# Second attention: weighed sums and the chain behind them moved in a software pipeline on one Trainium2 core

## The reference, cut to what matters

```python
q = query @ q_w + q_b; k = query @ k_w + k_b; v = query @ v_w + v_b
k = concatenate([k, bias_k]); v = concatenate([v, bias_v])        # 129 keys
w = einsum('bth,bsh->bts', q * scaling / 32, k)                   # per head
gate = sigmoid((query_layer @ grep_w + grep_b).sum(-1)) * grep_a
w = w + gate * rel_emb[buckets]
probs = softmax(w); attn = einsum('bts,bsh->bth', probs, v)
x = layernorm(x + attn @ out_w + out_b)
```

## Time and profile before

| what | value |
|---|---|
| median of 3 runs | 5380.33 us (5378.53 to 5382.32) |
| the profiled execution | 5384.48 us, span 5382.7 us |
| PE busy, granted clock over the span | 4154.7 us (77%), 0.77 |
| DVE busy | 3559.9 us (66%) |
| ACT busy | 2231.5 us (41%) |
| POOL busy | 1734.5 us (32%) |
| last `turn_rows` of the block | starts 3321.2 us |

### The profile page before, as it was taken

One profiled execution on the slowest core, in us unless ns is written; L12 is line 12 of the kernel. 1 busy time (PEld: TensorE's weight loads), 2 busy tenths in 40 slices (PEclk: granted clock), 3 DMA queues, 4 the chain that ended last, 5 costly groups with the idle time before them and its releaser, 6 DMA issues. The chain is left out here.

```text
span 5382.7 us, 100296 instructions
## 1 busy us (share of the span) xinstructions
PE 4154.7 (77%) x31987; PEld 2750.2 (51%) x31987; DVE 3559.9 (66%) x9085; ACT 2231.5 (41%) x5050; POOL 1734.5 (32%) x2290
## 2 busy tenths in 40 slices
PE   7878888878885666655989998777773299999998
PEld 3555555555554455443666666666663144444443
DVE  6565655645554555545888887555556688888888
ACT  1444444431111222214777776222221155555555
POOL 1000000015451000004565665000000077777777
PEclk9999999986555555556777776666665599999999
DMA  2000000000000000001000000111111365666664
GB/s 62 9 8 8 8 8 10 8 17 26 27 26 27 23 23 23 23 18 38 15 14 15 15 14 12 29 29 29 30 29 37 92 150 138 137 137 137 137 137 98
DMA packets 261713, 245.06 MB, mean 46 GB/s; under 512 B 28491, under 2 KB 188016, under 8 KB 261490
## 3 DMA queue, kind: packets, MB, share of 16 engines
q1 hardware_dynamic: 252402, 239.73, 18.5%
q10 hardware_dynamic: 9216, 4.20, 0.3%
HBM read 210.27 MB, written 33.55 MB: 45 GB/s over the span
## 5 line engine op out<-in xcount | busy, mean ns | idle before, releaser
L2314 POOL TENSOR_TENSOR d_hidden<-d_gated,d_upper 128x512 f32<-128x512 f32 x528 | 801.8, 1544 | 235.8 <-DVE d_upper L2423 110.5
L2430 DVE TENSOR_TENSOR d_h_low<-d_hidden,d_h_high 128x512 f16<-128x512 f32 x528 | 540.9, 1024 | 118.8 <-ACT d_h_high L2390 117.6
L2384 ACT ACTIVATE d_gated<-d_g 128x512 f32<-128x512 f32 x528 | 315.2, 597 | 468.3 <-PE d_u L2330 468.3
L2423 DVE TENSOR_TENSOR d_upper<-d_u,d_coef 128x512 f32<-128x512 f32 x512 | 349.1, 682 | 35.5 <-DMA d_coef<-coefT 16.3
L2390 ACT ACTIVATE d_h_high<-d_hidden 128x512 f16<-128x512 f32 x528 | 328.4, 622 | 8.2 <-POOL d_hidden L2314 8.2
L1563 ACT ACTIVATE c_sc<-c_sc,c_negmax 128x129 f32<-128x129 f32 x1024 | 326.2, 393 | 12.1 <-issue 9.7
L706 POOL MEMSET f_minus_half<- 128x1 f32 x1 | 0.1, 99 | 1027.4 <-POOLq L37 1027.4
L129 POOL TENSOR_TENSOR b_rstd<-b_var_eps,b_minus_half 128x1 f32<-128x1 f32 x128 | 67.1, 549 | 665.7 <-DVE b_var_eps L119 665.7
L1391 POOL TENSOR_TENSOR c_posg<-w_pos,c_gate 128x512 f32<-128x512 f32 x256 | 265.7, 1039 | 0.0
L2328 PE MATMUL d_g<-d_x_high,w_Wg_high 128*128 128x512 f16 x528 | 200.7, 380 | 79.0 <-DVE d_upper L2423 40.7
L129 POOL TENSOR_TENSOR d_rstd<-d_var_eps,d_minus_half 128x1 f32<-128x1 f32 x64 | 34.0, 547 | 682.0 <-DVE d_var_eps L119 682.0
(11 more groups left out here) (407 smaller groups left out, 11380.3 us busy)
## 6 DMA issues: line engine op xcount, KB each, us to landing
d_coef<-coefT SPq DMA_DIRECT2D x256, 512.0 KB, 7.6
mx_x<-in_xT SPq DMA_DIRECT2D x16, 256.0 KB, 2.8
b_x<-in_x SPq DMA_DIRECT2D x64, 64.0 KB, 1.8
y<-b_y SPq DMA_DIRECT2D x64, 64.0 KB, 1.6
f_y<-y SPq DMA_DIRECT2D x64, 64.0 KB, 1.9
f_x<-in_x SPq DMA_DIRECT2D x64, 64.0 KB, 1.9
x<-f_res SPq DMA_DIRECT2D x64, 64.0 KB, 1.5
b_x<-x SPq DMA_DIRECT2D x64, 64.0 KB, 1.8
```

The costliest lines, as they stand in the source:

```text
L2314: nc.gpsimd.tensor_tensor(hidden[b][:], gated[b][:], upper[b][:], ALU.mult).then_inc(h_ready, 1)
L2384: nc.scalar.activation(gated[b][:], ps_g[i][:], ACT.Silu, scale=1.0 / W_SCALE).then_inc(silu_ready, 1)
L2423: nc.vector.tensor_tensor(upper[b][:], ps_u[i][:], coef[c % CBUFS][:, u % CU, :], ALU.mult).then_inc(upper_ready, 1)
L2430: nc.vector.tensor_tensor(h_low[b][:], hidden[b][:], h_high[b][:], ALU.subtract).then_inc(h_low_ready, 1)
```

## The change: what it does

On PE, `weigh` goes from quarter 3 of the next column (`behind1`) to quarter 1 of the one after (`behind2`), between the turn of quarter 3 and `project`, which so comes behind `scores` and `turn`. `combine` goes to quarter 2, `turn_attn` to quarter 3 and `output` to quarter 0 of `behind3`. On ACT and DVE the parts that belong to them move along. On POOL `power` moves to quarter 1 of `behind3`, and the second product of `choose` becomes `last_values`, behind `low_parts`, with a wait for `pv_ready` of the item 4 places earlier, whose tile it writes over. `bn_stats` counts on a semaphore of its own, `bn_ready`, instead of the shared one.

```diff
@@ POOL @@
                     nc.gpsimd.tensor_tensor(chosen[s][:], following_kv[s][:, 1], own_next, ALU.mult).then_inc(chosen_ready, 1)
-                    nc.gpsimd.tensor_tensor(vlast_rows[s][:, :, 0:HD], following_kv[s][:, 0], own_next, ALU.mult).then_inc(vlast_ready, 1)
+
+                def last_values(it, j):
+                    s = slot(j)
+                    if not is_early(it, j, U):
+                        pool.wait_ge(pv_ready, nth(it, j) - U)
+                    nc.gpsimd.tensor_tensor(vlast_rows[s][:, :, 0:HD], following_kv[s][:, 0], w["own_next"][:].unsqueeze(2).to_broadcast([T, H, HD]),
+                                            ALU.mult).then_inc(vlast_ready, 1)
...
                     if a == 3:
                         run(low_parts, ahead2)
+                        run(last_values, ahead2)
...
                     if a == 1:
                         run(gates, ahead1)
-                    if a == 3:
-                        run(power, behind2)
+                        run(power, behind3)
@@ PE @@
                         run(gates_and_values, ahead1)
-                        run(combine, behind2)
+                        run(output, behind3)
                     if a == 1:
-                        run(project, ahead2)
                         run(scores, column, 2)
                         run(turn, behind1, 3)
-                        run(turn_attn, behind2)
+                        run(weigh, behind2)
+                        run(project, ahead2)
                     if a == 2:
                         run(scores, column, 3)
                         run(turn, column, 0)
-                        run(output, behind2)
+                        run(combine, behind2)
                     if a == 3:
                         run(scores, ahead1, 0)
                         run(turn, column, 1)
                         run(turn_last, behind1)
-                        run(weigh, behind1)
+                        run(turn_attn, behind2)
@@ ACT @@
                     if a == 0:
-                        run(copy_weighed, behind2)
...
                         run(gates_and_values, ahead1)
-                        run(norm, behind3)
                     if a == 1:
                         run(exps, column, 0)
                         run(copy_turned, behind1, 3)
-                        run(copy_attn, behind2)
-                        run(store, behind3)
                     if a == 2:
+                        run(copy_weighed, behind2)
                         run(exps, column, 1)
                         run(high_parts, ahead2)
                         run(copy_turned, column, 0)
+                        run(norm, behind3)
                     if a == 3:
                         run(exps, column, 2)
                         run(copy_turned, column, 1)
                         run(copy_last, behind1)
+                        run(copy_attn, behind2)
+                        run(store, behind3)
@@ DVE @@
-                    m = own.mark(nc.vector.bn_stats(bn[s][:], y[s][:]))
-                    own.wait(m)
+                    nc.vector.bn_stats(bn[s][:], y[s][:]).then_inc(bn_ready, 1)
+                    dve.wait_ge(bn_ready, nth(it, j))
...
                         run(bias, column, 0)
-                        run(normalise, behind2)
+                        run(add_x, behind3)
...
                         run(last_score, ahead1)
                         run(choose, ahead2)
-                        run(add_x, behind2)
                     if a == 3:
                         run(bias, column, 3)
+                        run(normalise, behind2)
                         run(turn_rows, ahead2)
```

More of the change, by code:

```diff
@@ L1266, in phase_attn1 @@
                  "gate_done", "posg_ready", "scores_ready", "biased", "top_ready", "exp_ready", "pT_ready", "pT_copied", "last_placed", "kv_next_ready",
-                 "lastT_ready", "lastT_copied", "pv_ready", "attn_ready", "attnT_ready", "attnT_copied", "out_ready", "x_biased_ready", "x_added", "mv_ready",
+                 "lastT_ready", "lastT_copied", "pv_ready", "attn_ready", "attnT_ready", "attnT_copied", "out_ready", "x_biased_ready", "x_added", "bn_ready", "mv_ready",
                  "rstd_ready", "offset_ready", "x4_ready", "own_front", "var_ready", "gate_added", "gate_ready", "last_bias_ready", "gate_inverted", "own_quarters", "own_back", "waited", "pool_waited", "low_ready", "rhs_ready", "chosen_ready", "weighed_ready", "weighed_copied")
@@ L1270, in phase_attn1 @@
          gate_done, posg_ready, scores_ready, biased, top_ready, exp_ready, pT_ready, pT_copied, last_placed, kv_next_ready,
-         lastT_ready, lastT_copied, pv_ready, attn_ready, attnT_ready, attnT_copied, out_ready, x_biased_ready, x_added, mv_ready,
+         lastT_ready, lastT_copied, pv_ready, attn_ready, attnT_ready, attnT_copied, out_ready, x_biased_ready, x_added, bn_ready, mv_ready,
          rstd_ready, offset_ready, x4_ready, own_front, var_ready, gate_added, gate_ready, last_bias_ready, gate_inverted, own_quarters, own_back, waited, pool_waited, low_ready, rhs_ready, chosen_ready, weighed_ready, weighed_copied) = (ph.sem(n) for n in names)
@@ L1687, in add_x @@
                 def add_x(it, j):
-                    s, own = slot(j), back_own
+                    s = slot(j)
                     dve.wait_ge(out_ready, nth(it, j))
```

## The result

The changed kernel takes 5436.4 us (median of 4 runs, 5435.0 to 5439.2), the kernel before 5379.4 beside it: ratio 1.0109, 95% interval 1.0091 to 1.0126. The change makes the kernel 57 us slower; the forecast was 5438.

A forecast was written before the change was run, and what follows sets the result against it. Bound: the loop of rows, gates, PE up to the projections and DVE from `project` to the rows. Columns of 14.55 against 13.63 over 60 give +55 us, the tail +3: 5380.3 becomes 5438, range 5355 to 5480.

The forecast's parts named there:

- The loop: Second attention: rows, gate columns, PE up to the projection, then DVE from `project` to the rows set each column.
- The PE part at the low level: From the start of `bias` 0 to DVE's `project`, all at low clock: 7.52 us against 5.81 before, 1.71 later.
- From DVE's `project` to the next `bias` 0: Rest of the column, added up along DVE: 7.71 us against 8.55, saving `add_x` with its wait less `normalise`.
- The clock: Level rises somewhere inside PE's weighed sums and projections; low work of 4.28 costs 2.92 to 4.28, middle 3.60; column 14.55.
- The tail: End of the block: the last but one item's weighed sums stand behind the column's last turn, +3 us.
- The other covers: Moved work on DVE, POOL, ACT and DMA stays hidden: -0.1 to +0.5 us a column, taken as 0.
- high from the first weighed sum: First rival, PE's weigh and project stretch: clock high from its start, column 13.21, total 5358, faster; chance 0.22.
- Rival 3: Level does not rise before the projections end, or turn 3 comes late: column 15.23, total 5479; chance 0.12.
- Rival 2: Clock changes fall in with column length and settle favourably: column 13.65 to 13.87, total 5384 to 5397; chance 0.18.

The follow-up runs named there:

- projections first: Changed kernel with PE's projections moved first in quarter 1, ahead of scores, turn 3 and the weighed sums: 5340.1 us, ratio 0.9934.
- power early: The kernel with projections first, and POOL's `power` moved ahead of `gates` in quarter 1: 5333.2 us, ratio 0.9916 to the kernel before.
- filling: Idle 128x128 f32 matmuls added on PE where it would wait: changed kernel with eight a column 5344.5 us, kernel before with five 5340.6 us.
- 8 idle matmuls in the better order: Projections first with power early, plus eight idle 128x128 f32 matmuls a column on PE (six and two): 5255.6 us, ratio 0.9772.
- weighed sums first: Changed kernel with PE's quarter 1 ordered weighed sums, projections, scores, turn 3: 5389.3 us, ratio 1.0024 to the kernel before.

## Why the prediction was right, point by point

- **The loop** is shown as predicted up to DVE's `choose`: rows, gates, PE up to the projections, DVE from `project` on. Reordering PE's quarter 1 alone moves the total by up to 104 us; work outside the loop is free (5433.6 against 5436.4), work inside is paid (5484.8). Its last part I had on the wrong engine: not DVE's `bias` 3 and `normalise` end last before the rows but ACT's high and POOL's low parts, by about 0.14 us.
- **The PE part at the low level**: predicted 7.52, measured 7.84 (3067.11 to 3074.95). Scores, weighed sums and projections came as taken from the rows; `output` took 0.70 instead of 0.56 and turn 3 1.04 instead of 0.90. Both were 0.14 too small: from one matmul group's start to the next it took that much longer in the new neighbourhood. Why was not tried.
- **From DVE's `project` to the next `bias` 0**: predicted 7.71, measured 7.45. The step from `bias` 3 to `normalise` fell from 2.00 to 1.52, since `negmax` took 0.17 and not 0.64: it no longer falls beside POOL's gated bias. That `negmax` takes longer beside POOL's gated bias is borne out by two runs: with projections first the 57 that began with 0.9 us of the gated bias still to come took 0.92 or 0.93, and with power early all but one (0.88) took 0.17 to 0.46. From `normalise` to `turn_rows` it took 0.72 instead of 0.50, because `turn_rows` waits for POOL's low parts. The prediction put their slack at 0.48 and counted nothing, and that sum is wrong: it took off 0.96 for `add_x` but not its wait, which leaves too. With the 1.34 of the sum before it, the slack is 0.94 - 1.34 + 0.50 = 0.10, and the faster `negmax` used it up.
- These misses cancel, 15.29 against 15.23. The method was right and the sum luckier than its terms: the 7.71 was added up along DVE, and the chain over ACT and POOL happened to take nearly as long.
- **The clock**: its rise inside the stretch, taken at the middle, gave a mean start of `project` of 6.84; measured 7.05, with 6.53 and 7.84 as ends. Column 14.55 against 14.51. It rose inside the dense stretch in three columns of four and behind it in the fourth: 4.84, 5.33, 6.28 and 7.92 us after `bias` 0, with columns of 13.99, 14.15, 14.61 and 15.29. That the level is the cause of the spread, filling shows: with 8 idle matmuls in the better order, where the clock is 1.00 from 2900 to 3100, the columns take 11.4 to 11.7 but for the first, and without them 12.2 to 13.4 but for one of 11.8. That it would come as a fixed round of four lengths I had not foreseen. What exactly lifts the level stays open.
- **The tail** was put at +3; measured 7.5, and 1.9 more for the fill. The block grew by 62.4 us in the traces and the forecast was 58, so that the median of 5436.4 falls within 2 us of 5438 is luck as well.
- **The other covers** held: no wait of DVE for combine, none for ACT in front of turn 3 but one of 1.4. POOL's new wait in `add_bias` came (59.2 us over 59 columns, about 1.0 each where I had 0.8) and cost nothing.
- **The rivals**: high from the first weighed sum is refuted for this kernel by the 0.50 row, and made true by filling in most columns (weighed sums 1.08 us, then 0.91 and 0.59 for the projections). Rival 3's column, low to the end of the projections, came once in four. Rival 2's price did not come here; equal columns came only in the run with weighed sums first, at 13.65.

## What to carry to other kernels

In a software pipeline, ask of every instruction moved on an in-order engine what now stands behind it: the weighed sums could come half a column later without a wait on DVE, the projections behind them could not (143.5 us of waits). Put the producer of the loop's next wait first in its quarter, and let work with slack follow; that one line was worth 96 us. And where TensorE's idle time is not on the path, look at the granted clock: work that is thrown away may pay, here 39 to 92 us. And a chain that leaves an engine and comes back, here from DVE over ACT and POOL, can bind with gaps too short for a list of waits, here 0.03 to 0.04 us: compare the end of the producer with the start of the consumer.

## What the runs showed of the hardware that I had not expected

Added matmuls made three kernels faster: by 92 us in the changed order, 39 in the old one, 60 and 78 (5 and 8 a column) in the better order with power early. A fall of the level costs a single column 3 us (15.35 against 12.33): the one that starts at 3039.43 ran at 0.50 from 3042.35 to 3048.95, and its idle matmuls at 1.00. And the lengths of columns fall into a pattern with the clock's changes: 13.65 each with the weighed sums first, a round of four in the changed kernel. That the clock ties them is argued from these lengths and was not tested.
